# Moving the first batch's maxima, the query products and the weight pieces in the prologue of an attention and expert kernel

## The chip, the cores and the metric

The kernel runs on one core of a Trainium2 chip. The metric is the device time of one execution in microseconds. Engines are named as the profile names them: PE (matmuls; PEld its weight loads), DVE, ACT, POOL (elementwise work), SP (issues most DMAs). Each works through its own queue in order; semaphores join them.

## What is computed

One transformer layer for 8 batches of 512 tokens of width 256, with a context of the same shape. Of the reference, cut:

```
h   = layernorm(x)                                  # 8 x 512 x 256
qp  = h @ Wq.T                                      # query product
idx = argmax(qp @ ctx.T, axis=-1)                   # scores: each token chooses one context row
mk, mv = split(ctx[idx] @ Wkv.T)                    # 16 wide each, shared by all 16 heads
attn = softmax(qh @ mk.T / 4)                       # 16 heads of width 16
x   = x + tanh(g0) * ((attn @ mv) merged @ Wc.T)
h   = layernorm(x)
gate = h @ gate_w                                   # best 2 of 8 experts, softmax weights
x   = x + tanh(g1) * sum over the 2 of w * (gelu(h @ w1 + b1) @ w2 + b2)
```

## The kernel before

Only chosen context rows matter as keys, so the kernel counts how often each is chosen, packs the used ones into 192 slots and weights them by their counts. For each batch the work goes through these steps, in the names of the code and the trace:

- DVE's statistics of x (`x_stats`), POOL's `rstd` and normalising (`x_in`), PE's transposes (`turn_x`), ACT's copy (`turned`);
- PE's query product, two halves of 128 columns (`project`, into `ps_e0` and `ps_e1`), ACT's copy of each half (`q_t`), ACT's high halves (`query_hi`), POOL's low halves (`query_lo`), and SP's store of both (`queries`) and load into the stacked form `q_st` (`stack`, which holds SP until the load has landed);
- PE's scores, four tiles; DVE's search of each (MAX8 and FIND_INDEX8, `top`, `top_at`), and a mask of the chosen rows (`chosen_keys`: on DVE for the first batch, on POOL for the others);
- PE's counts, DVE's used keys, PE's ranks, DVE's positions, POOL's `values` and `places` (places on DVE for the first batch), PE's packing (`pack`, L1263 and L1268), ACT's `packed_keys`, which writes `k_st` and `v_st`;
- the maxima: 32 tiles of 128 x 384 logits (`logits_b`, L1280, bf16), of which DVE takes the row maxima (`take_max`, L987, `row_max`); then DVE splits them, PE turns them, DVE copies them (`max_t`) and SP stores them into the last rows of the stack (`store_max`), so that the next logits come out with the maximum subtracted;
- the logits (L1300, L1304), ACT's exponentials (L805), PE's weighted sums (L1317), then the layer's output, the gate and the scatter to expert queues. After all batches come the experts.

The order is written out by hand. All engines run the same loop over p = −4 to 7 and 32 steps each (`each_step`); a batch has its x loaded in p = b − 4, its query product in p = b − 3, its scores to packing in p = b − 2, the second part of its maxima in p = b − 1 and its logits in p = b. A table of step numbers for each engine (L407 to L427) says at which step an engine issues what; in one step the order is that of the `if`s in the engine's loop. Maxima tiles go one a step, beginning 7 steps before the end of p = b − 2 (`MAX_EARLY`), so that 7 tiles of a batch stand before the step in which the batch before has its first logits. While p < 0 the tiles and the scores go round four PSUM banks (`ps_d0, ps_d1, ps_a0, ps_a1`); from p = 0 the tiles have `ps_d` alone and the logits `ps_a` (`ring`). A tile can't be written before DVE has read the one four places earlier.

The experts' weights are brought in by 32 pieces of 512 KB: SP loads one into one of two stages (`load_piece`), ACT casts its high half (`piece_hi`, L849), POOL subtracts the low half (`piece_lo`, L706, 128 x 1024). `W_AT` gives the step of `piece_hi` for some p, POOL's follows one step later, SP's load of the piece after the next three steps later, which waits until the low half has freed the stage. DVE also copies the gate's 8 columns into a wide tile (`gate_wide`) before its loop, for which it waits for `tanh_g`.

## Time and profile before

| | |
|---|---|
| three runs | 923.81, 924.6, 925.47 us |
| median | 924.6 us |
| profiled execution | 923.9 us, its span 922.1 us |
| PE, DVE, ACT, POOL busy | 87%, 56%, 40%, 46% |

The span runs from the first to the last instruction; the profiled execution's time has 1.8 us more around it. Rows of the timeline give a start and a duration in us, and in brackets how long the engine had been idle and what ended that. The chain of waits is followed back from the last instruction, so that its rows add up to the span. Times in both are from the start of the span.

### The profile page before, as it was taken

The numbers are of one execution on the slowest core, as the hardware profiler recorded it, in microseconds if no ns is written. First come the engines' busy times: TensorE is split into PE (matmuls) and PEld (weight loads), VectorE is DVE, ScalarE is ACT, GpSimd is POOL, SyncE is SP. The second block draws the span as 40 slices with busy tenths as digits, with TensorE's granted clock in tenths as the row PEclk, the third lists the DMA queues.
The fourth block names the chain that finished last, engine by engine and source line by source line (L and its number), as shares of the span: only waits on it lengthen the run. The fifth ranks groups of instructions, "written<-read, shape, count | busy, mean of one in ns | idle before, by whom it ended". The sixth has DMA issues, their size and how long they took to land.

```text
span 922.1 us, 20046 instructions
## 1 busy us (share of the span) xinstructions
PE 801.9 (87%) x6326; PEld 547.1 (59%) x6327; DVE 521.0 (56%) x1582; ACT 370.3 (40%) x772; POOL 427.6 (46%) x469
## 2 busy tenths in 40 slices
PE   3785899989897998888778868999999999999994
PEld 1333344435353443443347657899888888899773
DVE  4585576667767567776444873544444544444441
ACT  1222363735435363566653612433333333333331
POOL 4596363755666546443614753333333333333322
PEclk9886899979899898989989989999999999999998
DMA  5554333353624334224425342322222333322300
GB/s 173 129 122 139 60 92 80 117 104 93 128 95 109 64 114 105 69 70 136 138 88 160 54 127 46 59 47 46 44 46 44 55 53 50 48 42 36 44 12 1
DMA packets 62798, 74.64 MB, mean 81 GB/s; under 512 B 6401, under 2 KB 56449, under 8 KB 62593
## 3 DMA queue, kind: packets, MB, share of 16 engines
q1 hardware_dynamic: 49424, 56.74, 24.0%
q0 software_dynamic: 13296, 16.92, 10.7%
q8 instruction: 42, 0.69, 0.3%
q14 instruction: 36, 0.29, 0.1%
HBM read 46.75 MB, written 27.55 MB: 81 GB/s over the span
## 4 chain that ended last, share of the span: by engine, by line
PE 66%; DVE 12%; ACT 6%; issue 6%; POOL 5%; DMA 3%; DVEq 1%; SPq 1%; ACTq 0%; POOLq 0%
PE ps_o L2578 20%; PE ps_d L2562 9%; PE ps_a L2562 9%; PE ps_d L1237 6%; PE ps_o L1317 5%; PE ps_d L1280 3%; PE ps_e L1212 3%; PE ps_e L1342 3%; PE ps_a L1300 2%; PE ps_e L1195 2%; DVE row_max L987 2%; PE ps_r L2548 1%; ACT prob L805 1%; ACT rows L827 1%; PE ps_a L1304 1%
## 5 line engine op out<-in xcount | busy, mean ns | idle before, releaser
L2578 PE MATMUL ps_o<-w_split,hidden 128*128 x1136 | 192.2, 276 | 13.4 <-DVE y L2534 8.4
L805 ACT ACTIVATE prob<-ps_a 128x512 f32<-128x512 f32 x192 | 112.9, 603 | 188.0 <-PE ps_a L1300 109.8
L987 DVE TENSOR_REDUCE row_max<-ps_d 128x2 f32<-128x384 f32 x237 | 127.8, 551 | 58.8 <-PE ps_d L1280 57.4
L2578 PE MATMUL ps_o<-w_split,h_lo 128*128 x568 | 156.6, 276 | 0.0
L2473 POOL DMA_INDIRECT out<-y,token_at x71 | 118.5, 1669 | 42.3 <-POOL token_at L2471 30.9
L2578 PEld LDWEIGHTS ps_o<-w_split,hidden 128*128 128x128 bf16 x1136 | 112.1, 99 | 30.2 <-issue 15.3
L2520 DVE TENSOR_TENSOR h_lo<-hidden 128x512 bf16<-128x512 f32 (+1 forms) x156 | 101.0, 686 | 25.5 <-ACT hidden L2489 24.7
L2534 DVE TENSOR_TENSOR y<-ps_o,b_all 128x512 f32<-128x512 f32 (+1 forms) x39 | 25.1, 644 | 155.6 <-PE ps_o L2578 148.7
L1280 PE MATMUL ps_d<-k_st,w_split 96*128 96x192 bf16 x474 | 84.4, 267 | 26.4 <-DVE row_max L987 19.8
L2562 PE MATMUL ps_a<-x_hi,w_split 128*128 128x256 bf16 (+1 forms) x624 | 104.4, 265 | 0.0
L2562 PE MATMUL ps_d<-x_hi,w_split 128*128 128x256 bf16 (+1 forms) x624 | 103.6, 264 | 0.1
L2469 POOL TENSOR_TENSOR token_f<-tails,ones_f 128x2 f32<-128x2 f32 (+1 forms) x39 | 7.7, 197 | 206.0 <-DVE y L2537 203.7
L706 POOL TENSOR_TENSOR w_split<-w_stage,w_split 128x1024 bf16<-128x1024 f32 x32 | 68.9, 2177 | 54.8 <-ACT w_split L849 54.8
L2480 ACT CAST x_hi<-ps_r 128x512 bf16<-128x512 f32 (+1 forms) x39 | 21.4, 548 | 168.6 <-PE ps_r L2548 168.6
L2489 ACT ACTIVATE hidden<-ps_d,bias 128x256 f32<-128x256 f32 (+1 forms) x156 | 62.4, 452 | 62.1 <-PE ps_d L2562 62.1
L1280 PEld LDWEIGHTS ps_d<-k_st,w_split 96*128 96x128 bf16 x474 | 39.7, 103 | 78.2 <-DVE row_max L987 31.9
L2562 PE MATMUL ps_a<-x_lo,w_split 128*128 128x256 bf16 (+1 forms) x312 | 81.9, 263 | 0.0
L1317 PE MATMUL ps_o<-prob,v_st 128*32 128x512 f32 x512 | 76.8, 675 | 5.5 <-issue 4.1
L2562 PE MATMUL ps_d<-x_lo,w_split 128*128 128x256 bf16 (+1 forms) x312 | 81.4, 263 | 0.0
L2489 ACT ACTIVATE hidden<-ps_a,bias 128x256 f32<-128x256 f32 (+1 forms) x156 | 62.4, 452 | 35.5 <-PE ps_a L2562 35.5
L700 POOL DMA_INDIRECT queue<-rows,slot x64 | 63.9, 999 | 19.4 <-issue 17.1
L2562 PEld LDWEIGHTS ps_a<-x_hi,w_split 128*128 x624 | 60.7, 97 | 9.4 <-issue 1.2
(242 smaller groups left out, 1307.1 us busy)
## 6 DMA issues: line engine op xcount, KB each, us to landing
w_stage<-w SPq DMA_DIRECT2D x32, 512.0 KB, 4.5
xg<-queue SPq DMA_DIRECT2D x31, 260.0 KB, 2.9
w_split<-q_split SPq DMA_DIRECT2D x24, 256.0 KB, 8.0
x_in<-x SPq DMA_DIRECT2D x8, 512.0 KB, 4.3
ctx_sb<-ctx_t SPq DMA_DIRECT2D x8, 512.0 KB, 3.9
x<-x SPq DMA_DIRECT2D x8, 512.0 KB, 4.3
q_split<-q_hl SPq DMA_DIRECT2D x16, 256.0 KB, 3.4
out<-x SPq DMA_DIRECT2D x8, 512.0 KB, 5.0
```

Of the source, the lines that this page charges most:

```text
L700: pool.indirect_dma_start(k.queue[:], bass.IndirectOffsetOnAxis(ap=slot[:, t, c:c + 1], axis=0), rows[:, t, :], None).then_inc(scattered, 16)
L706: g.tensor_tensor(lo, stage, hi, ALU.subtract).then_inc(w_lo, 1)
L805: a.activation(prob[n % 2][:, j, :], ps_a[i % 2][:], ACT.Exp, scale=SCALE).then_inc(exp_ready, 1)
L987: v.tensor_reduce(row_max[:, t, 2 * pair:2 * pair + 2], bank[:, 0:2 * SLOTS].rearrange("p (h r) -> p h r", h=2), AX.X, ALU.max).then_inc(m ...
L1237: last = t_.matmul(ps_da[n][:], q_t[:, kt, t * P:(t + 1) * P], ctx_sb[:, kt, :], start=(kt == 0), stop=(kt == KT - 1))
L1280: last = t_.matmul(ps_da[n][:, c * SLOTS:(c + 1) * SLOTS], q_st[m % 3][0:ROW_MAX, 2 * pair + c, t * P:(t + 1) * P], k_st[0:ROW_MAX, m % 3, ...
L1317: last = t_.matmul(ps_o[j * VW:(j + 1) * VW, :], values, probs, start=(key_tile == 0), stop=(key_tile == SLOT_TILES - 1))
L2473: pool.indirect_dma_start(k.out_rows, bass.IndirectOffsetOnAxis(ap=token_at[:, t:t + 1], axis=0), y[s][:, t, :], None, bounds_check=B * L ...
L2489: last = nc.scalar.activation(hidden[s][:, f, 0:width(i)], ps_h[n][:, c, 0:width(i)], ACT.Gelu, bias=bias[s][:, f:f + 1])
L2520: nc.vector.tensor_tensor(h_lo[s][:, both, tokens], hidden[s][:, both, tokens], h_hi[s][:, both, tokens], ALU.subtract).then_inc(h_lo_read ...
L2562: last = nc.tensor.matmul(ps_h[n][:, c, 0:width(i)], k.w1_split[:, bass.ds(e, 1), part, kt, f].rearrange("p a f -> p (a f)"), xs[s][:, kt, ...
L2578: last = nc.tensor.matmul(ps_y[:, t, :], hs[s][:, f, token], k.w2_split[:, bass.ds(e, 1), part, f, :].rearrange("p a d -> p (a d)"), start ...
```

## The change

The sizes and the number of instructions stay. The first batch's maxima go two tiles a step for the first 12 steps and then one a step (`FIRST_MAX`), still from the 26th step of p = −2 on, so that they end in step 12 of p = −1; their split, turn, copy and store move from steps 25 to 28 into steps 13 to 16 (`max_steps`). For p < 0 the query product's halves move from steps 16 and 17 to 19 and 25, behind ranks (18), and behind packing (22) for the second half; ACT's copies, high halves, POOL's low halves and SP's store follow (`query_steps`). In p = −2 and −1 ACT's high halves of the weight pieces move from steps 4, 10, 18, 26 to 13, 15, 22, 28, and with them POOL's low halves and SP's loads. The gate columns move from ahead of DVE's loop into p = −3.

```diff
-        W_AT = {-2: (4, 10, 18, 26), -1: (4, 10, 18, 26), 6: (4, 10, 18, 26), 7: (2, 8, 14, 20)}
+        W_AT = {-2: (13, 15, 22, 28), -1: (13, 15, 22, 28), 6: (4, 10, 18, 26), 7: (2, 8, 14, 20)}
...
+        def query_steps(p):
+
+            return ((19, 25), (20, 26), 27, 28, 29) if p < 0 else (PE_PROJECT, ACT_QUERY, ACT_QUERY_HI, POOL_QUERY_LO, SP_QUERIES)
+
+        def max_steps(m):
+
+            return (13, 14, 14, 16) if m == 0 else (DVE_SPLIT_MAX, PE_TURN_MAX, DVE_COPY_MAX, SP_MAX)
...
-        def max_tile(p, step):
+        FIRST_MAX = [2] * 12 + [1] * 8
+
+        def max_tiles(p, step):
 
             m, tile = divmod(p * STEPS + step + MAX_EARLY, STEPS)
-            return (m + 1, tile) if is_batch(m + 1) else None
+            if m >= 0:
+                return [(m + 1, tile)] if is_batch(m + 1) else []
+            n = (p + 1) * STEPS + step + MAX_EARLY
+            return [(0, sum(FIRST_MAX[:n]) + i) for i in range(FIRST_MAX[n])] if 0 <= n < len(FIRST_MAX) else []
...
-                if step == SP_QUERIES and is_batch(p + 3):
+                if step == query_steps(p)[4] and is_batch(p + 3):
                     queries(p + 3)
...
-                if step == SP_MAX and is_batch(m):
+                if is_batch(m) and step == max_steps(m)[3]:
                     store_max(m)
...
-                if step == POOL_QUERY_LO and is_batch(p + 3):
+                if step == query_steps(p)[3] and is_batch(p + 3):
                     query_lo(p + 3)
...
-            dve.wait_ge(dve_ready, 2)
-            dve.wait_ge(pool_ready, 1)
-            dve.wait_ge(tanh_ready, 1)
-
-            chain.then(v.memset(gate_wide[:], 0.0))
-            v.tensor_copy(gate_wide[:, :, 0:E], k.gate_sb[:]).then_inc(dve_ready, 1)
+            def gate_columns():
+                dve.wait_ge(pool_ready, 1)
+                dve.wait_ge(tanh_ready, 1)
+                chain.then(v.memset(gate_wide[:], 0.0))
+                v.tensor_copy(gate_wide[:, :, 0:E], k.gate_sb[:]).then_inc(dve_ready, 1)
...
             n_d = 0
+            dve.wait_ge(dve_ready, 2)
             for p, step in each_step():
...
+                if step == 0 and p == -3:
+                    gate_columns()
...
-                row_tile = max_tile(p, step)
-                if row_tile:
+                for row_tile in max_tiles(p, step):
                     take_max(*row_tile, (ps_d + ps_a)[ring(p, n_d)][:])
                     n_d += 1
...
-                row_tile = max_tile(p, step)
-                if row_tile:
+                for row_tile in max_tiles(p, step):
                     logits_b(*row_tile, ring(p, n_d))
                     n_d += 1
...
-                if step in PE_PROJECT and is_batch(p + 3):
-                    project(p + 3, PE_PROJECT.index(step))
+                if step in query_steps(p)[0] and is_batch(p + 3):
+                    project(p + 3, query_steps(p)[0].index(step))
```

ACT's queries and high halves, the split, the copy and the turn of the maxima are edited in the same way. The changed file's lines are 13 or 14 higher.

How the order moves is seen at three places. On PE, from the counts of the first batch (`chosen`) through the second batch's query product (`wq_sb`), ranks (`used`) and packing (`key_cols`, `value_cols`) to the first maxima tiles (`k_st`, two matmuls a tile), before:

```order
L1247 MATMUL ps_r<-ones_bf,chosen 128x1 x16
L1212 MATMUL ps_e<-turned,wq_sb 128x512 x4
L1255 MATMUL ps_r<-used,before 128x4
L1256 MATMUL ps_r<-used,ones_bf 128x4
L1263 MATMUL ps_e<-chosen,key_cols 98x192 x4
L1268 MATMUL ps_e<-value_cols,chosen 128x17 x8
L1268 MATMUL ps_e<-value_cols,chosen 64x17 x16
L1280 MATMUL ps_d<-k_st,w_split 128x192 x4
```

and after:

```order
L1261 MATMUL ps_r<-ones_bf,chosen 128x1 x16
L1269 MATMUL ps_r<-used,before 128x4
L1270 MATMUL ps_r<-used,ones_bf 128x4
L1226 MATMUL ps_e<-turned,wq_sb 128x512 x2
L1277 MATMUL ps_e<-chosen,key_cols 98x192 x4
L1282 MATMUL ps_e<-value_cols,chosen 128x17 x8
L1282 MATMUL ps_e<-value_cols,chosen 64x17 x16
L1294 MATMUL ps_d<-k_st,w_split 128x192 x4
L1226 MATMUL ps_e<-turned,wq_sb 128x512 x2
```

The ranks stand directly behind the counts, half of the product ahead of packing, and the other half behind the first two maxima tiles. Behind it come 23 more tiles before the second batch's first scores (25 in all; before, 13 tiles stood ahead of them); the same pattern stands in p = −1, there with the second half of the product behind the first tile of the second batch. On ACT, from the second batch's `turned` to the first batch's packed keys (`k_st`, `v_st`), before:

```order
L760 COPY turned<-ps_e 128x512
L761 COPY turned<-ps_e 128x512
L768 COPY q_t<-ps_e 128x512 x2
L849 CAST w_split<-w_stage 128x1024
L774 CAST q_hl<-q_t 128x2x512
L780 ACTIVATE k_st<-ps_e,key_add,key_mul 98x192
```

and after:

```order
L773 COPY turned<-ps_e 128x512
L774 COPY turned<-ps_e 128x512
L862 CAST w_split<-w_stage 128x1024
L781 COPY q_t<-ps_e 128x512
L862 CAST w_split<-w_stage 128x1024
L793 ACTIVATE k_st<-ps_e,key_add,key_mul 98x192
```

The third weight piece's cast (the second cast shown after) stands directly ahead of the packed keys, and the second copy and the high halves of the queries behind them. On POOL, from the choice of the second batch's last tiles (`best`, `chosen<-column,best`) to its places (`chosen<-column,position`), before:

```order
L648 TENSOR_SCALAR chosen<-column,best 128x512
L706 TENSOR_TENSOR w_split<-w_stage,w_split 128x1024
L647 CAST best<-top_at 128x1
L648 TENSOR_SCALAR chosen<-column,best 128x512
L652 TENSOR_TENSOR value_f<-kv,count 128x4x16
L654 COPY value_f<-count 128x4
L657 CAST value_cols<-value_f 128x4x17
L658 TENSOR_TENSOR value_cols<-value_f,value_cols 128x4x17
L706 TENSOR_TENSOR w_split<-w_stage,w_split 128x1024
L668 TENSOR_SCALAR chosen<-column,position 128x192 x4
```

and after:

```order
L660 CAST best<-top_at 128x1
L661 TENSOR_SCALAR chosen<-column,best 128x512
L719 TENSOR_TENSOR w_split<-w_stage,w_split 128x1024 x2
L665 TENSOR_TENSOR value_f<-kv,count 128x4x16
L667 COPY value_f<-count 128x4
L670 CAST value_cols<-value_f 128x4x17
L671 TENSOR_TENSOR value_cols<-value_f,value_cols 128x4x17
L681 TENSOR_SCALAR chosen<-column,position 128x192 x4
```

Two weight pieces stand between the last choice and the values, and none between the choices or ahead of the places. On SP the loads of the second batch's context and the third batch's x stand ahead of two weight pieces behind the first stack; before, they stood second and fourth of the four.

## Rows read from the trace of the kernel before

**Rows 1.** Chain that ended last, 0 to 130: start, us, what
```profile
31.95 8.00 DMA w_split<-q_split
...
40.96 0.46 SPq L515
...
67.35 2.08 POOL w_split L706
...
78.70 2.12 POOL w_split L706
...
80.82 2.97 POOL chosen L668 x4
...
83.83 0.88 PE ps_e L1263 x4
...
89.40 3.09 DMA w_split<-max_t
...
92.54 0.61 PE ps_a L1300
...
98.69 1.93 PE ps_d L1237 x4
```

**Rows 2.** Timeline: start, us, engine line op out<-in [idle <-releaser]; the start
```profile
3.69 6.95 POOL L636 MEMSET w_split<- 96x4096 f32 x2
...
11.38 0.24 POOL L673 TENSOR_SCALAR variance<-moments 128x4 f32<-128x4 f32 x1 [0.74 <-DVE moments L1023]
```

**Rows 3.** Timeline, to the first batch's first maxima tile, 39 to 49 us
```profile
39.17 5.95 PE L1212 MATMUL ps_e<-turned,wq_sb 128*128 128x512 f32 x8
...
45.63 1.05 ACT L849 CAST w_split<-w_stage 128x1024 bf16<-128x1024 f32 x1
...
47.98 0.51 ACT L780 ACTIVATE k_st<-ps_e,key_add,key_mul 98x192 bf16<-98x192 f32 x1 [0.36 <-PE ps_e L1268]
...
48.89 0.49 PE L1280 MATMUL ps_d<-k_st,w_split 96*128 96x192 bf16 x4 [0.95 <-issue]
```

**Rows 4.** DMA issues near 41 us: count, KB each, us to landing
```profile
ctx_sb<-ctx_t SPq DMA_DIRECT2D x1, 512.0 KB, 4.7
w_stage<-w SPq DMA_DIRECT2D x1, 512.0 KB, 5.6
```

**Rows 5.** Timeline, maxima tiles, second batch's scores, 49 to 68 us
```profile
49.87 0.99 DVE L987 TENSOR_REDUCE row_max<-ps_d 128x2 f32<-128x384 f32 x2
...
54.72 3.28 PE L1237 MATMUL ps_d<-ctx_sb,q_t 128*128 128x512 f32 x4
...
55.42 0.56 DVE L987 TENSOR_REDUCE row_max<-ps_d 128x2 f32<-128x384 f32 x1
...
58.04 0.70 DVE L945 MAX8 top<-ps_d 128x8 f32<-128x512 f32 x1 [2.07 <-PE ps_d L1237]
...
67.09 0.69 DVE L946 FIND_INDEX8 top_at<-top,ps_a 128x8 uint32<-128x512 f32 x1
```

**Rows 6.** Timeline, choice, third batch's product, values, 69 to 75 us
```profile
69.67 1.56 POOL L648 TENSOR_SCALAR chosen<-column,best 128x512 bf16<-128x512 f16 x1
...
72.01 3.13 PE L1212 MATMUL ps_e<-turned,wq_sb 128*128 128x512 f32 x4
...
73.17 0.29 POOL L652 TENSOR_TENSOR value_f<-kv,count 128x64 f32<-128x64 f32 x1 [1.94 <-DVE used L958]
...
73.99 0.31 POOL L658 TENSOR_TENSOR value_cols<-value_f,value_cols 128x68 bf16<-128x68 f32 x1
```

**Rows 7.** Busy time by stretch; third from last: PE's granted clock
```profile
54.00:55.00 1.00, 0.95 (x5) 0.44 (x4) 1.00 (x4) 0.00 (x0) 1.00 (x2) 0.50 0.00 0
...
72.00:73.00 1.00, 1.00 (x4) 0.48 (x3) 0.71 (x3) 0.00 (x0) 0.00 (x0) 0.50 1.04 395
...
99.00:100.00 1.00, 1.00 (x3) 0.38 (x2) 0.00 (x0) 0.00 (x0) 0.00 (x0) 1.00 1.17 116
```

**Rows 8.** Timeline, the second batch's first maxima tiles, 86 us
```profile
86.64 0.80 PE L1280 MATMUL ps_d<-k_st,w_split 96*128 96x192 bf16 x4 [0.20 <-issue]
```

More of the change, by code:

```diff
@@ L857, in _ @@
                     turned_x(p + 3)
-                if step in ACT_QUERY and is_batch(p + 3):
-                    query(p + 3, ACT_QUERY.index(step))
-                if step == ACT_QUERY_HI and is_batch(p + 3):
+                if step in query_steps(p)[1] and is_batch(p + 3):
+                    query(p + 3, query_steps(p)[1].index(step))
+                if step == query_steps(p)[2] and is_batch(p + 3):
                     query_hi(p + 3)
@@ L1128, in _ @@
                     x_moments_of(p + 4)
-                if step == DVE_SPLIT_MAX and is_batch(m):
+                if is_batch(m) and step == max_steps(m)[0]:
                     split_max(m)
-                if step == DVE_COPY_MAX and is_batch(m):
+                if is_batch(m) and step == max_steps(m)[2]:
                     copy_max(m)
@@ L1420, in _ @@
                     turn_rows(e)
-                if step == PE_TURN_MAX and is_batch(m):
+                if is_batch(m) and step == max_steps(m)[1]:
                     turn_max(m)
```

## Prediction

> **What bounds the kernel now.** The change touches only what runs before the first logits, so that stretch alone is read, first in the chain of waits from 0 to 130 us [rows 1]. The reader is to see how often the step that ends last there is a single DMA or one engine's queue: the stack load that holds SP until 31.95 + 8.00 = 39.95, the weight pieces of POOL at 67.35 and 78.70, the placing of the second batch's keys at 80.82, the packing at 83.83, the store of the first batch's maxima at 89.40, and the first logits at 92.54. The timelines then give durations. I cut the stretch at six points: first maxima tile on PE 48.89 [rows 3]; first MAX8 of the second batch's scores 58.04; end of the fourth search, 67.09 + 0.69 = 67.78 [rows 5]; packing 83.83; first logits 92.54; third batch's first scores 98.69 [rows 1]. The stages last 48.9, 9.1, 9.7, 16.1, 8.7 and 6.2 us. From 98.69 on both kernels issue the same rows, and what waits there waits for its predecessors and not for the clock on the wall, so a shift at 98.69 is carried to the end whole.
>
> **Stage 1, start to the first tile.** The gate columns no longer hold DVE for tanh_g. What is late next is POOL: its memsets end at 3.69 + 6.95 = 10.64, and the variance that started at 11.38 [rows 2] can start some 0.7 us earlier, no more. Query products and ranks are exchanged: before, the first batch's ranks stood behind the second batch's whole product (39.17, 5.95 for eight records, [rows 3]); now half of it, about 3 us, stands there, and behind the ranks. Packing can so begin near 44, by half the product and a copy behind 39.17. But ACT has the third weight piece in its queue ahead of the packed keys, and that piece is loaded third after the stack: SP is free at 39.95 less the 0.35 that I take of the 0.7 (the low halves on POOL now stand behind two normalised tiles), 39.6; the third transfer is issued 1.0 later (40.96 against 39.95, [rows 1]) and lands 5.6 after its issue [rows 4]: 46.2. The cast takes 1.05, so the key copy starts at 47.3 instead of 47.98, and the tile 0.91 behind it as before (48.89 − 47.98, [rows 3]): 48.2. **−0.7 us**; 0 if the load starts no earlier. The x of the third batch moves from fourth to second in line (4.7 after issue, [rows 4]), so its statistics no longer hold the first maximum.
>
> **Stage 2, first tile to the second batch's first search.** PE had 13 tiles ahead of the first scores and now has 25. DVE's pitch is (55.42 + 0.56 − 49.87)/13 = 0.47 us a tile [rows 5], and PE keeps ahead of it even at half clock (0.80 for two tiles at 86.64, [rows 8]), so 12 more cost 5.6. Behind the first two tiles stands the second half of the query product, four records, on which DVE waits in full. At 72.01 such four took 3.13 [rows 6] at a granted clock of 0.50, that is 1.2 GHz [rows 7]; the same shape at full clock took 1.93 (98.69, [rows 1], clock 1.00 at 99). PE is nearly idle from about 45.5 to 48.2, as it was before 72.01, so I take 3.1. Gained back is DVE's late start: 49.87 came 0.98 behind the tile, now about 0.4, −0.6. **+8.1 us**, down to +6.9 with the product at full clock. The first scores ran at half (54.72, 3.28, clock 0.50); I leave them so; at full they give 1.35 back.
>
> The Trainium skill, "TensorE: Matmul & The Clock Gate", Part 1, says that the throttled state is the default and that sustained activity releases it, so that products behind an idle stretch start at half rate. The clock at 72 agrees. The rule speaks against a product set between two idle stretches; by it both moved halves run at half clock, and without it the sum below would be 2.4 us less.
>
> **Stage 3, the four searches.** DVE has the same rows in the same order with seven tiles between and behind: 0.
>
> **Stage 4, last search to packing, 16.05 us before.** POOL's choice of the fourth tile was held by a weight piece (67.35, 2.08), the ranks by the whole product, and the placing by another piece (78.70, 2.12). Now the choice follows at once, 1.56 [rows 6] and with the copy ahead of it and hand-overs 1.9; then come two weight pieces in a row, 2 x 2.12 = 4.25; values, 73.99 + 0.31 − 73.17 = 1.13 [rows 6]; placing 2.97 [rows 1]; hand-overs 0.3. Sum 10.55. Counts and used keys (POOL waited 1.94 for them at 73.17), then ranks and positions, hide behind the two pieces, and half the product (3.1) and its copy behind pieces, values and placing. ACT's high half of the second piece waits for the turned x, which PE issues about with the last search: ready before POOL wants it. **−5.5 us**, ±0.5. Were the pieces not there, values would start about 3 us earlier; this is the cover that the change doesn't give.
>
> **Stage 5, packing to the first logits, 8.71 before.** Packing to the first tile of the second batch stays 86.64 − 83.83 = 2.81 [rows 1, 8]. The maxima are stored long before, which takes the 3.09 of the store out of the chain. But behind that first tile now stands the other half of the third batch's product (0.4 + 3.1), and behind it six tiles whose maxima DVE must take before the bank of the logits is free: 0.45 to the first, 0.55 for it, 5 x 0.47. Sum 9.7: **+1.0 us**; with the product at full clock −0.2.
>
> **Stage 6, first logits to the next scores, 6.15 before**, all at half clock until 98. The product just ahead may bring PE's clock up. At full clock I bound the gain between 0 and 2.0 (a third of the stage; its exponentials and hand-overs don't shrink), and take **−0.9**, since tiles alone between 49 and 54 didn't hold the clock up (0.50 at 54, [rows 7]).
>
> Weight pieces moved cost the SP queue nothing else: the maxima's store waits on SP behind the context and x loads, which are issued before the maxima exist. The second batch's stack now waits for one more piece's low half, and is issued near 61 and loaded some nine later, 18 us before its first tile.
>
> **Sum:** −0.7 + 8.1 + 0 − 5.5 + 1.0 − 0.9 = **+2.0 us**. The profiled execution took 923.9 us (span 922.1, 1.8 around it); the median of the three shown is 924.6. 923.9 + 2.0 = 925.9, and against the median **926.6 us**. About 0.2%, 1.85 us, is what a measurement of this kernel can tell from no change.
>
> **The rivals.** *Same, by the clock:* the product of stage 5 and the first logits run at full clock: −0.7 + 8.1 − 5.5 − 0.2 − 2.0 = −0.3, 924.3 us. For it: four records of f32 work at 72 were followed by full clock. Against it: six tiles follow, and at such tiles the clock fell to half by 54. *Same, by the piece:* the third weight piece lands earlier than I have it, so that the key copy follows packing. Then the tile is near 46.4 instead of 48.2, and the sum +0.2: 924.8 us. Against it: the transfers before it landed one behind the other [rows 4]. *Faster:* PE holds the full clock from the first packing on. Then stage 2 loses 1.2 and 1.35, stage 5 another 1.2, stage 6 the whole 2.0: −0.7 + 5.5 − 5.5 − 0.2 − 2.0 = −2.9, 921.7 us. It decides where the product behind the second tile takes under 2.5 us and the first scores under 2.6. Against it are PE's idle stretches on both sides of packing. *Slower still:* the second scores run at half too (+1.35) and nothing comes back in stage 6 (+0.9): +4.3, 928.9 us. *The change doesn't do what it says:* the first tile comes no sooner, since the piece's landing decides; this is in the forecast.
>
> **How the numbers follow.** The forecast gets 0.40, slower still 0.08, the two that end the same 0.28 and 0.08, faster 0.16. So faster by over 0.2% 0.16, within 0.2% 0.36, slower by over 0.2% 0.48. Slower and same hold most of the chance; the forecast's own range, from stage 6 at −2.0 to stages 1 and 6 at 0, is 925.5 to 928.2. The range that leaves out no more than 2 in 10 reaches from 922.0, which takes in most of the faster case by its milder clocks, to 929.8, above the worst case by the ±0.5 of stage 4 and some.
>
> **What would show it.** Right: the key copy directly behind a weight cast that waited for its load, near 47.3; 25 tiles at 0.47 with a hole of about 3 us behind the second; the first search near 65.5; two weight pieces between POOL's last choice and the values; the maxima's store landed by about 81; first logits near 95.4. Wrong: the key copy before 46, the first search before 63.5, or values that start before the second piece; and a first-logits time that isn't carried to the end.

## The result, and the profile after

The kernel before has a median of 925.1 us over seven runs, the three above and four more. The changed kernel takes **928.2 us** (seven runs, 927.7 to 930.7), a ratio of **1.0047**, 95% interval 1.0037 to 1.0058: slower by some 4.3 us by this ratio and by 3.0 us by the medians, where 2.0 was forecast. Its profiled execution took 929.6 us, its span 927.9.

The chain of waits of the changed kernel from 40 to 106 us (start, us, what; line numbers 12 to 14 higher than before). It answers [rows 1]:

```profile
45.19 3.43 issue
48.62 0.80 PE ps_d L1294 x4
49.42 3.47 PE ps_e L1226 x4
...
62.77 3.75 PE ps_d L1251 x4
...
77.22 1.56 POOL chosen L661
78.78 2.18 POOL w_split L719 x2
...
84.21 3.00 POOL chosen L681 x4
87.26 0.53 PE ps_e L1277 x4
...
90.18 3.49 PE ps_e L1226 x4
...
97.05 0.39 PE ps_a L1314
...
102.98 2.90 PE ps_d L1251 x4
```

The store of the maxima of 89.40 [rows 1] is gone from the chain. The stack load of 31.95 isn't listed in it either, but it still decides: the 3.43 us of "issue" are PE's wait for the first batch's key copy, which stands on ACT behind a cast that waited 3.49 us for its weight piece (46.76 and 47.71 below), and SP could issue that load only behind the stack's, after 39.92. New in the chain are half products, at 49.42 behind the first two tiles and at 90.18 behind the second batch's first; the two weight pieces at 78.78 stand in a row. The timeline has what waits behind these (idle time and its cause in brackets), and answers [rows 3, 5, 6]:

```profile
39.92 0.38 SPq L556 DMA_DIRECT2D ctx_sb<-ctx_t  x1
...
46.76 1.04 ACT L862 CAST w_split<-w_stage 128x1024 bf16<-128x1024 f32 x1 [3.49 <-DMA w_stage<-w]
...
47.71 0.51 ACT L793 ACTIVATE k_st<-ps_e,key_add,key_mul 98x192 bf16<-98x192 f32 x1
...
53.24 1.02 DVE L999 TENSOR_REDUCE row_max<-ps_a 128x2 f32<-128x384 f32 x2 [3.08 <-PE ps_a L1294]
...
66.56 0.70 DVE L957 MAX8 top<-ps_d 128x8 f32<-128x512 f32 x1 [2.54 <-PE ps_d L1251]
...
79.14 0.84 SPq L570 DMA_DIRECT2D w_split<-max_t  x1
...
94.03 0.56 DVE L999 TENSOR_REDUCE row_max<-ps_d 128x2 f32<-128x384 f32 x1 [3.25 <-PE ps_d L1294]
```

DVE's two idle times of 3.08 and 3.25 us, both released by a tile behind a half product, are the holes. The clock in single microseconds (third from last) answers [rows 7]:

```profile
49.00:50.00 1.00, 1.00 (x4) 0.59 (x3) 0.87 (x2) 0.00 (x0) 1.00 (x2) 0.50 0.00 0
...
54.00:55.00 1.00, 0.75 (x7) 0.23 (x4) 1.00 (x3) 1.00 (x2) 0.34 (x1) 1.00 0.00 0
62.00:63.00 1.00, 0.94 (x5) 0.39 (x4) 1.00 (x3) 0.00 (x0) 0.00 (x0) 0.50 0.68 70
...
95.00:96.00 1.00, 0.38 (x3) 0.11 (x2) 1.00 (x4) 1.00 (x2) 0.55 (x1) 1.00 0.00 0
99.00:100.00 1.00, 1.00 (x6) 0.28 (x3) 0.73 (x2) 0.85 (x2) 1.00 (x2) 0.50 0.99 351
103.00:104.00 1.00, 1.00 (x2) 0.48 (x3) 0.00 (x0) 0.00 (x0) 0.00 (x0) 0.50 0.96 123
```

Behind each half product the clock was up (1.00 at 54 and 95), and each time it was back at 0.50, which is 1.2 GHz, before the next scores: at 62 under tiles, at 99 under the first logits. Both half products and the first scores of the second batch ran at half, those of the third batch until near 105.

Cut at the six points of the prediction, the stages of every kernel run, as differences from the kernel before, in us, from one profiled execution each (the sixth cut is the start of PE's first record, 98.62 before). The last columns: all up to there; up to the MAX8 of the third batch's first scores (100.64 before); and of the runs the median and the ratio to the kernel before. The ratio is the recorded one, against runs of the kernel before from the same session (medians 924.9 to 925.2); it differs from the quotient of the medians by up to 0.14%, 1.3 us. One execution carries its own clock: in *gate columns only* no row of the scores was edited, yet the second batch's first scores are 0.5 us longer than before and the third batch's 1.8 us. Differences of that size in a single stage need a second sign.

| kernel | 1 | 2 | 3 | 4 | 5 | 6 | sum | MAX8 | median | ratio |
|---|---|---|---|---|---|---|---|---|---|---|
| forecast | −0.7 | +8.1 | 0 | −5.5 | +1.0 | −0.9 | +2.0 | | 926.6 | |
| changed | −0.3 | +8.8 | +0.6 | −5.7 | +1.1 | −0.2 | +4.3 | +5.3 | 928.2 | 1.0047 |
| gate columns only | −0.7 | +1.6 | +0.7 | +0.3 | 0.0 | +0.2 | +2.2 | +4.0 | 924.7 | 0.9999 |
| pieces only | +0.1 | −0.6 | +0.4 | −3.6 | +1.5 | +0.2 | −1.9 | −1.3 | 923.5 | 0.9971 |
| tiles only | −0.3 | +6.5 | +0.2 | −0.2 | −1.9 | +0.2 | +4.5 | +5.4 | 931.2 | 1.0071 |
| product only | −0.9 | +3.3 | +0.2 | −4.1 | +1.3 | −0.7 | −1.1 | −1.0 | 923.6 | 0.9996 |
| tiles undone | −0.3 | +1.2 | +0.2 | −5.4 | +2.3 | 0.0 | −2.1 | −2.1 | 924.2 | 0.9988 |
| pieces undone | −1.6 | +8.2 | +0.2 | −5.2 | +1.1 | +0.2 | +2.8 | +3.1 | 928.1 | 1.0037 |
| product undone | −0.6 | +5.6 | +0.8 | −5.7 | −2.4 | +0.2 | −2.0 | −1.1 | 924.6 | 0.9991 |
| product ahead of packing | 0.0 | +5.5 | +0.8 | −5.6 | −2.2 | +0.2 | −1.4 | −0.6 | 921.5 | 0.9972 |
| changed, PE kept busy | −1.3 | +6.6 | +0.6 | −5.7 | −1.2 | +0.2 | −0.8 | −0.6 | 923.5 | 0.9984 |
| late pairs | −0.4 | −0.4 | +0.3 | −4.1 | −1.9 | +0.2 | −6.3 | −5.4 | 919.0 | 0.9927 |
| late pairs, four added | +3.0 | −0.1 | +0.7 | −4.1 | −2.7 | +0.2 | −3.0 | −2.7 | 914.9 | 0.9889 |
| late pairs, three added | −0.7 | −0.7 | 0.0 | −2.9 | −2.6 | +0.2 | −6.8 | −6.0 | 916.2 | 0.9911 |

### The profile page after: what moved, and what is told of

It is laid out like the page before. It is cut to its first block, busy times and chain, and to the rows that moved or that the text cites. A ratio compares the mean times of both kernels' runs of the same rounds, so it can differ in the third digit from the quotient of the medians.

```text
span 927.9 us, 20045 instructions
## 1 busy us (share of the span) xinstructions
PE 811.0 (87%) x6326; PEld 549.7 (59%) x6327; DVE 524.5 (57%) x1582; ACT 369.8 (40%) x772; POOL 427.4 (46%) x469
## 3 DMA queue, kind: packets, MB, share of 16 engines
HBM read 46.75 MB, written 27.55 MB: 80 GB/s over the span
## 4 chain that ended last, share of the span: by engine, by line
PE 69%; DVE 14%; ACT 6%; issue 6%; POOL 4%; DVEq 1%; DMA 0%; ACTq 0%; POOLq 0%
PE ps_o L2591 20%; PE ps_d L2575 9%; PE ps_a L2575 8%; PE ps_d L1251 6%; PE ps_o L1331 5%; PE ps_e L1226 4%; PE ps_d L1294 3%; PE ps_e L1356 3%; DVE row_max L999 3%; PE ps_a L1314 2%; PE ps_e L1209 2%; PE ps_r L2561 1%; ACT prob L818 1%; DVE top_at L958 1%; PE ps_a L1318 1%
## 5 line engine op out<-in xcount | busy, mean ns | idle before, releaser
L2591 PE MATMUL ps_o<-w_split,hidden 128*128 x1136 | 194.9, 278 | 11.6 <-DVE y L2547 6.7
L1294 PEld LDWEIGHTS ps_d<-k_st,w_split 96*128 96x128 bf16 x474 | 39.6, 103 | 81.2 <-DVE row_max L999 32.7
```

The lines of the kernel that those rows point to most:

```text
L1294: last = t_.matmul(ps_da[n][:, c * SLOTS:(c + 1) * SLOTS], q_st[m % 3][0:ROW_MAX, 2 * pair + c, t * P:(t + 1) * P], k_st[0:ROW_MAX, m % 3, ...
L2591: last = nc.tensor.matmul(ps_y[:, t, :], hs[s][:, f, token], k.w2_split[:, bass.ds(e, 1), part, f, :].rearrange("p a d -> p (a d)"), start ...
```

## The experiments

The first four undo one part of the change, or all but one.

**Tiles undone** (the rest as changed):

```diff
-        FIRST_MAX = [2] * 12 + [1] * 8
+        FIRST_MAX = [1] * 32
...
-            return (13, 14, 14, 16) if m == 0 else (DVE_SPLIT_MAX, PE_TURN_MAX, DVE_COPY_MAX, SP_MAX)
+            return (25, 26, 27, 28) if m == 0 else (DVE_SPLIT_MAX, PE_TURN_MAX, DVE_COPY_MAX, SP_MAX)
```

> The changed kernel with one edit undone: the first batch's maxima go one tile a step again and their store stands where it stood before. Theory (the twelve tiles ahead of the second batch's scores cost more than the earlier store gives back): the first search comes 12 x 0.47 = 5.6 us earlier than in the changed kernel, near 61.0; values and packing follow it, packing near 81.7; then the store of the maxima stands in the chain again and puts the first logits at about 8.7 to 10 us behind packing, 91 to 92. Against the kernel before -1 to 0 us (ratio 0.999 to 1.000), against the changed kernel some 4 us less. Rival 1 (the weight pieces cost it: the third one ahead of the packed keys, two ahead of the values): nothing of that is undone, so the time stays within 1 us of the changed kernel's, ratio near 1.004. Rival 2 (TensorE's clock: the products and first scores at half): the same, since both halves of the product still stand between idle stretches; ratio 1.003 to 1.005.

Measured: 924.2 us, ratio 0.9988 (0.9976 to 1.0000), 4.0 us under the changed kernel, as the theory had it; both rivals had at most 1 us. Its chain:

```profile
49.06 3.22 PE ps_e L1226 x4
...
56.90 1.95 PE ps_d L1251 x4
...
82.77 3.44 PE ps_e L1226 x4
...
87.32 3.11 DMA w_split<-max_t
```

The first scores come 5.9 us earlier, and here at full clock (1.95 for 3.75), so the first search is at 58.9 instead of 66.6: 5.6 by tiles, 1.8 by the clock. Both half products are still there, and behind the second one the store of the maxima is back in the chain: the stage before the first logits costs +2.3.

**Pieces undone:**

```diff
-        W_AT = {-2: (13, 15, 22, 28), -1: (13, 15, 22, 28), 6: (4, 10, 18, 26), 7: (2, 8, 14, 20)}
+        W_AT = {-2: (4, 10, 18, 26), -1: (4, 10, 18, 26), 6: (4, 10, 18, 26), 7: (2, 8, 14, 20)}
```

> The changed kernel with the weight pieces back at their old steps; maxima and products stay as changed. Theory: the key copy no longer stands behind the third piece's cast (46.76 in the changed kernel), so the first tile reaches PE near 46 instead of 48.6; the third batch's x is loaded last again, so its statistics hold DVE until some 50 us, under which the 3-us hole behind the second tile disappears: DVE is through the tiles 1 to 2.5 us earlier. Later POOL's pieces stand between the choices and ahead of the places again, which costs part of it back: 0 to +1.5 in the stage from the last search to packing. In all -1 to -2.5 us against the changed kernel, ratio to the kernel before 1.002 to 1.003. Rival (the pieces are what costs the 4 us): all of it comes back, ratio 0.999 to 1.001. Rival (the tiles alone cost it, pieces are neutral): ratio 1.004 to 1.005.

Measured: 928.1 us, ratio 1.0037 (1.0024 to 1.0050); by the medians nothing, by the stages 1.5 us less than changed, nearly all from the first tile, which comes at 47.26. The hole of 3 us behind the second tile stayed (PE's half product 48.05, 3.14, DVE's next maxima at 51.39), which the theory had hidden. The rival that the pieces cost the 4 us falls. Unlooked for was the fourth stage: with the pieces back between the choices and ahead of the places it still gained 5.2.

**Product undone:**

```diff
-            return ((19, 25), (20, 26), 27, 28, 29) if p < 0 else (PE_PROJECT, ACT_QUERY, ACT_QUERY_HI, POOL_QUERY_LO, SP_QUERIES)
+            return (PE_PROJECT, ACT_QUERY, ACT_QUERY_HI, POOL_QUERY_LO, SP_QUERIES) if p < 0 else (PE_PROJECT, ACT_QUERY, ACT_QUERY_HI, POOL_QUERY_LO, SP_QUERIES)
```

> The changed kernel with the query product for p < 0 back ahead of the ranks, both halves together; tiles, store and pieces stay as changed. Theory (each moved half is an uncovered wait of 3.0 to 3.5 us on DVE, once behind the second tile of the first batch and once behind the first tile of the second): the first search comes 3 us earlier, near 63.5, and the stretch from packing to the first logits is 3 us shorter, near 6.8; the ranks stand behind the whole product again, which costs 0 to 3 us between the last search and packing where two weight pieces cover most of it. In all -3 to -6 us against the changed kernel, ratio to the kernel before 0.998 to 1.001. Rival (tiles cost it, the product is neutral as it only changes places): ratio 1.004 to 1.005. Rival (clock: the product in one piece brings PE to full clock for the tiles and scores behind it): first scores under 2.6 us and ratio under 0.998.

Measured: 924.6 us, ratio 0.9991 (0.9976 to 1.0006), 3.6 us under the changed kernel by the medians and 6.3 by the stages. The holes are gone (second stage +5.6, about the twelve tiles, with first scores of 3.75; fifth −2.4, the store out of the chain), and the fourth stage keeps its −5.7, although the whole product stands ahead of the ranks again. The clock rival falls: the product in one piece did not keep the clock up until the scores.

**Gate columns only:** the three edits above together.

> Of the change only the gate columns' move from ahead of DVE's loop into p = -3; the rest is as in the kernel before. Every theory: POOL's variance starts at 10.6 instead of 11.4; how much of these 0.7 us reaches the first tile depends on the store and load of the first stack, between 0 (as in the changed kernel, where the stack landed as late as before) and 0.7. Ratio to the kernel before 0.9992 to 1.0005; above 1.002 the move of the gate columns itself would cost something that no theory has.

Measured: 924.7 us, ratio 0.9999 (0.9989 to 1.0009): nothing. In its profiled execution the first tile comes 0.7 earlier, and then the first scores run at 3.75 and the third batch's at 3.73 us; the 4.0 us that it is late at the MAX8 are gone at the end (923.4 against 923.9).

**One part alone.** Undoing the tiles and undoing the product each gave back nearly all; so the parts don't add up, and each was run alone. *Pieces only* (tiles and product undone):

> Of the change only the weight pieces and the gate columns; one maxima tile a step, their store and the query product as in the kernel before. Theory by stages: the gain of the stage from the last search to packing (-5.2 to -5.7 in every kernel so far that had any of the moved parts but the gate columns alone) comes with the pieces and needs nothing else; nothing is added ahead of the second batch's scores, where PE's clock decides between -1 and +1.6; packing to first logits as before. First tile near 48.3, packing near 78 to 80, first logits near 87 to 89, ratio to the kernel before 0.994 to 0.997. Rival (the gain needs the product out of the way of the ranks, or the tiles): packing near 83 to 84, ratio 0.999 to 1.001. Second rival (what the prologue gains or loses isn't carried to the end): packing near 79 but a ratio of 0.998 to 1.001.

Measured: 923.5 us, ratio 0.9971 (0.9957 to 0.9986). By the medians that is 1.4 us under the kernel before, by the ratio 2.7. The gain of the fourth stage is there without the other parts, but it is 3.6 and not 5.5: POOL had to wait for the places, as its timeline shows (POOL) with its chain (PE):

```profile
77.22 2.99 POOL L681 TENSOR_SCALAR chosen<-column,position 128x192 bf16<-128x192 f16 x4 [2.28 <-DVE position L981]
```

```profile
70.47 3.15 PE ps_e L1226 x4
...
73.95 1.88 PE ps_e L1226 x4
```

The first half of the product ahead of the ranks ran at half clock here (clock 0.50 from 71 to 73), so positions came 2.3 us behind POOL. In the kernel with only the product undone the clock was 1.00 from 65 to 83, and positions held POOL by 0.17 us.

*Tiles only* (pieces and product undone):

> Of the change only the maxima's tiles two a step with their store, and the gate columns; product and weight pieces as in the kernel before. Theory by stages: S2 +5.6 (12 tiles of 0.47), up to +1.5 more where the scores run at 3.75 instead of 3.28; S4 as before (16 us), since the pieces stand between the choices and ahead of the places; S5 -2.4, since the store is out of the chain; first logits near 95 to 97; ratio to the kernel before 1.002 to 1.005. Rival (two tiles a step and the earlier store pay for themselves, and the product alone is to blame): ratio 0.998 to 1.001.

Measured: 931.2 us, ratio 1.0071 (1.0056 to 1.0085), more than the theory's upper end; by the stages +4.5, by the MAX8 +5.4. The tiles are the costly part, and their rival falls.

*Product only* (tiles and pieces undone):

> Of the change only the query product's moved halves with what follows them, and the gate columns; tiles, store and weight pieces as in the kernel before. Theory by stages: S2 +1 to +3.5 for the half behind the first tile, less where the third batch's statistics on DVE cover it; S4 0 to -1.5, since the ranks come free but two pieces still stand in POOL's way; S5 +2.3, since the other half stands behind the second batch's first tile and the store of the maxima waits behind that; first logits near 93.5 to 96.5; ratio to the kernel before 1.002 to 1.005. Rival (the product is neutral by itself, and only with the pairs of tiles it costs): ratio 0.999 to 1.001.

Measured: 923.6 us, ratio 0.9996 (0.9979 to 1.0012), no difference, where the theory had 1.002 to 1.005. That is the rival's number but not its reason: the product isn't neutral. The second stage cost 3.3, as expected, and the fifth 1.3 instead of 2.3, but the fourth gave 4.1 instead of 0 to 1.5, with the pieces at their old places:

```profile
69.83 2.09 POOL w_split L719
...
72.15 1.59 POOL chosen L661
73.78 0.58 PE ps_r L1261 x16
...
76.88 2.04 DVE offset L980
...
79.20 3.01 POOL chosen L681 x4
```

Before, a whole product stood ahead of the ranks, positions came at 77.7, and POOL was then held by a piece until 80.82 [rows 1]. That piece was late because of the product too: its cast stood on ACT behind the copies of the product's halves, and POOL waited 4.40 us for it (timeline of the kernel before, ACT and POOL):

```profile
77.09 0.58 ACT L768 COPY q_t<-ps_e 128x512 f32<-128x512 f32 x1 [1.33 <-PE ps_e L1212]
77.57 1.05 ACT L849 CAST w_split<-w_stage 128x1024 bf16<-128x1024 f32 x1
...
78.70 2.12 POOL L706 TENSOR_TENSOR w_split<-w_stage,w_split 128x1024 bf16<-128x1024 f32 x1 [4.40 <-ACT w_split L849]
```

Moving the product frees the ranks and this cast; moving the pieces takes the piece out of the way. Without the product there, places begin 1.6 us earlier although the searches end 2.5 later. So most of the 5.5 us of the fourth stage can be had by moving the product *or* the pieces (4.1 and 3.6 alone, 5.2 and 5.7 with the tiles moved too); the second one to be moved adds little: with the tiles moved, 0.5 for the pieces, and 0 for the product, which ran at full clock there.

**Product ahead of packing** (else as changed):

```diff
-            return ((19, 25), (20, 26), 27, 28, 29) if p < 0 else (PE_PROJECT, ACT_QUERY, ACT_QUERY_HI, POOL_QUERY_LO, SP_QUERIES)
+            return ((19, 20), (20, 21), 22, 24, 25) if p < 0 else (PE_PROJECT, ACT_QUERY, ACT_QUERY_HI, POOL_QUERY_LO, SP_QUERIES)
```

> The changed kernel with the second half of the query product for p < 0 put behind ranks and the first half, ahead of packing, where the first half already stands; tiles, store and weight pieces stay as changed. Theory by stages (the cost of the product is where its halves stand, not how long they take): the holes of 3 us behind the first batch's second tile and behind the second batch's first tile go, as they went when the product was put back ahead of the ranks (S2 +5.6 instead of +8.8, S5 -2.4 instead of +1.1). The second half then stands ahead of packing in both batches: for the first one packing moves from 43.4 to about 47, so that the key copy follows it and no longer the third weight piece, 0 to +1.2 at the first tile; for the second the product of up to 7 us stands beside two weight pieces, values and places of 8.3 us together, 0 to +1. In all ratio to the kernel before 0.997 to 1.001. Rival (the product costs by its half clock wherever it stands): ratio 1.003 to 1.005.

Measured: 921.5 us, ratio 0.9972 (0.9957 to 0.9986). Both holes go and the fourth stage keeps its gain: it is the place of the second half behind the tiles that costs, not its length.

**Late pairs.** If twelve tiles ahead of the scores cost and the pieces leave DVE and PE idle later, the pairs belong there (product undone as above):

```diff
-        FIRST_MAX = [2] * 12 + [1] * 8
+        FIRST_MAX = [1] * 20 + [2] * 6
...
-            return (13, 14, 14, 16) if m == 0 else (DVE_SPLIT_MAX, PE_TURN_MAX, DVE_COPY_MAX, SP_MAX)
+            return (19, 20, 20, 22) if m == 0 else (DVE_SPLIT_MAX, PE_TURN_MAX, DVE_COPY_MAX, SP_MAX)
```

> The changed kernel with the query product for p < 0 back ahead of the ranks, and with the pairs of maxima tiles placed last instead of first: one tile a step until 20 are done (13 of them ahead of the second batch's first scores, as in the kernel before), then two a step for six steps, while the second batch's keys are chosen and the weight pieces split on POOL; the store of the maxima follows three steps later. Theory by stages: nothing is added ahead of the scores (0 to +1.6 by PE's clock instead of +5.6), the gain between last search and packing stays (-5 to -5.7), and the store is out of the chain of the first logits (-2.4). First logits near 84.5 to 87, ratio to the kernel before 0.991 to 0.995. Rival (late tiles only move the wait, as DVE takes 5.6 us of them beside the second batch's used keys and positions): packing 2 to 4 us later than that, ratio 0.996 to 0.999. Second rival (not carried): first logits near 86, ratio 0.998 to 1.001.

Measured: **919.0 us**, ratio **0.9927** (0.9908 to 0.9945), some 6.8 us under the kernel before by the ratio and 5.9 by the medians; first logits at 86.05. The theory holds but for the fourth stage, −4.1 instead of −5 to −5.7. The rival's mechanism, tiles beside the used keys, has a part in that, with another one on top. The timeline of *late pairs* (DVE and POOL):

```profile
71.57 1.84 DVE L970 TENSOR_SCALAR used<-count 128x4 bf16<-128x4 f32 x1
```

```profile
69.18 4.22 POOL L719 TENSOR_TENSOR w_split<-w_stage,w_split 128x1024 bf16<-128x1024 f32 x2
```

`used` over four columns takes 0.17 us elsewhere. Here it ends at 73.41, with POOL's two pieces (73.40), and the ranks, positions and places wait behind it.

**PE kept busy.** The clock's part is told by matmuls that nobody needs: in the changed kernel, two behind the first batch's packing and one ahead of the second's.

```diff
+            def filler(n):
+                for _ in range(n):
+                    t_.matmul(ps_o[:], wq_sb[:, 0, 0:P], turned[:, 0, :], start=True, stop=True)
...
                 if step == PE_PACK and is_batch(s):
+                    if s == 1:
+                        filler(1)
                     pack(s)
+                    if s == 0:
+                        filler(2)
```

> The changed kernel with three matmuls of the size of the query product's added on PE, into a bank that nobody reads before it is written anew: two behind the first batch's packing, while the key copy waits for a weight piece, and one ahead of the second batch's packing, while POOL places. Clock theory (the 3.5 us of each moved half and the 2.96 to 3.75 of the first scores are half-clock times that come from PE's idle stretches just ahead): with the stretches filled the half behind the second tile takes 1.9 to 2.5 instead of 3.5, first scores 1.9 to 2.6, and the half behind the second batch's first tile about 1.9: 2 to 4 us off the changed kernel, ratio to the kernel before 1.000 to 1.002. Rival (the clock doesn't rise for so few, or the time is set elsewhere): durations stay at 3.3 to 3.75, or the fillers delay packing by 0 to 1, ratio 1.004 to 1.006.

Measured: 923.5 us (916.7 to 928.4 in twelve runs), ratio 0.9984 (0.9960 to 1.0009), 4.7 us under the changed kernel. Its chain:

```profile
44.94 1.91 PE ps_o L1398 x4
...
48.10 1.75 PE ps_e L1226 x4
...
59.57 3.75 PE ps_d L1251 x4
...
86.53 1.83 PE ps_e L1226 x4
```

The half products take 1.75 and 1.83 instead of 3.47 and 3.49, as the clock theory has it, and the whole execution (920.5 us) had a mean granted clock of 0.951, where the changed kernel's seven had 0.935 to 0.942. But this trace doesn't show that the added matmuls brought the clock up. It had risen before the first of them (single microseconds, third from last the clock):

```profile
43.00:44.00 1.00, 0.28 (x5) 0.29 (x5) 0.00 (x0) 0.58 (x1) 0.00 (x0) 0.68 1.09 378
44.00:45.00 1.00, 1.00 (x28) 0.95 (x27) 0.76 (x3) 0.00 (x0) 0.00 (x0) 1.00 1.09 345
```

In the changed kernel it was 0.50 from 37 to 53, although PE has the same instructions up to there. That is a difference between the two executions; the added matmuls, 1.91 us between packing and the first tile, can at most have kept the clock up until the product. The first scores still took 3.75: tiles alone did not hold it up. The twelve executions go with the clock, but for one: with 0.951 to 0.954 four took 916.7 to 920.5, with 0.939 to 0.942 three took 926.9 to 928.4, and one with 0.946 took 926.9 as well. By medians the matmuls give back 4.7 us, more than the two products' 3.4 and as much as the whole loss, and the intervals of the two ratios don't overlap. That the added matmuls shorten the time is shown; that they do it by the clock at these two products rests on one trace.

**Late pairs with added matmuls,** two behind the first packing and two ahead of the second:

> The kernel with the late pairs of tiles (product ahead of the ranks, pairs last) and four added matmuls of the size of the query product's into a bank that nobody reads before it is written anew: two behind the first batch's packing, two ahead of the second batch's, both while PE waits. Clock theory: what the half clock still costs there (first scores 3.34 at 53.85, tiles 0.8 at 82.04, first logits and weighted sums from 86 to 95, all at 0.50) comes partly back: first scores 1.9 to 2.6, packing to first logits 5.5 to 6.5 instead of 6.82, first logits to the next scores 4.5 to 6 instead of 6.25; 1.5 to 4 us less than without them, ratio to the kernel before 0.988 to 0.992. Rival (the clock rises behind the added matmuls but tiles alone don't hold it until the scores, as with the fillers in the changed kernel, where the scores still took 3.75): 0 to 1.5 us, ratio 0.991 to 0.994.

Measured: **914.9 us** (914.5 to 922.1, five runs), ratio **0.9889** (0.9874 to 0.9903). The profiled execution was the one of 922.1, with a mean clock of 0.945; the others had 0.951 to 0.952. What it shows is a cost: the added matmuls ran at half and held the first tile back to 51.89 (chain; packing itself came only at 47.22, as the whole product ahead of it ran at half too):

```profile
48.45 3.61 PE ps_o L1398 x4
```

So that trace doesn't explain the median. The last kernel has one instead of two there:

> The kernel with the late pairs of tiles and the added matmuls, with one of them instead of two behind the first batch's packing (two stay ahead of the second batch's packing). In the profiled execution with two, the added ones ran at half clock (3.61 from 48.45) and held the first tile back to 51.89; its mean granted clock was 0.945 and its time 922.06, while the four others had 0.951 to 0.952 and 914.5 to 917.6. Clock theory: one takes 0.9 to 1.8 and ends ahead of the key copy, the first tile comes at 48.5 again, and the mean granted clock is 0.948 to 0.952 with a time of 0.988 to 0.991 of the kernel before. Rival (one is too little to bring the clock up, or the four executions were quick for another reason): mean granted clock 0.940 to 0.945 and ratio 0.991 to 0.994, as without any.

Measured: 916.2 us (915.8 to 918.1), ratio 0.9911 (0.9897 to 0.9925), mean clock 0.949 to 0.953 in all five, against 0.940 to 0.945 in the six of *late pairs*. The first tile is at 48.15. But up to the third batch's scores it gains only 0.4 us on *late pairs*, as the added matmuls ahead of the second packing cost about what they bring (chain):

```profile
47.20 1.05 PE ps_o L1398 x2
...
76.16 3.51 PE ps_o L1398 x4
79.66 0.43 PE ps_e L1277 x4
```

The rest of the 4.0 us between the two profiled executions lies later, in stretches where both issue the same rows. From 240 to 270 us *late pairs* and this kernel, in this order (third from last the clock):

```profile
240.00:270.00 30.00, 28.83 (x168) 14.48 (x161) 20.00 (x50) 10.47 (x19) 16.97 (x19) 0.87 0.35 74
```

```profile
240.00:270.00 30.00, 28.83 (x176) 14.43 (x175) 19.52 (x49) 10.70 (x20) 18.06 (x23) 1.00 0.40 115
```

Why added matmuls before 80 us should keep the clock up at 250 isn't shown by any run. The interval of the four lies just below that of *late pairs* without any, that of the three overlaps with it.

## Why the prediction was right in sign and short in size

*The mechanism* was right: 25 tiles ahead of the scores, holes behind the moved halves, two pieces in a row, and the store out of the chain. The first search was put at 65.5 and came at 66.6, the first logits at 95.4 and came at 97.05. The 2.3 us that the sum lacks at the sixth cut are four terms, each short by half a microsecond or so. That the cut's +4.3 equals the 4.3 us by the ratio is partly chance: the profiled executions lie 1.5 us above the median of the changed kernel and 1.2 below that of the kernel before.

- *Stage 1, −0.7 forecast, −0.3 measured.* POOL's variance started at 10.64, 0.74 earlier, as forecast. But SP was free for the next loads at 39.92 instead of 39.6: the store of the queries was issued 0.5 us earlier (27.55 for 28.05) and the load of the stack behind it 0.2 later (31.27 for 31.06): the gain was lost between the store's issue and its landing (2.7 us at the median, 2.3 before). The cast waited for its load, and the key copy stood right behind it, as foreseen (46.76, 47.71; forecast 47.3 for the copy).
- *Stage 2, +8.1 forecast, +8.8 measured.* The pitch of 0.47 held. The half product stood 3.47 us in the chain instead of 3.1: at 72.01 [rows 6] the clock had risen before the product ended (0.77 in the microsecond from 74), here it did not. The scores took 3.75 instead of 3.28 for the same reason: before [rows 5], the clock rose from 57 on, while they ran.
- *Stage 3, 0 forecast, +0.6 measured.* The same rows in the same order, but PE's keys and values (L1236) ran at half clock, 0.84 in the chain. Where they did (0.81 to 1.01, *gate columns only*, *product undone* and *PE kept busy* among them), the stage is 0.6 to 0.8 longer; where they took 0.57, it is between 0 and 0.4. The step left the clock out.
- *Stage 6, −0.9 forecast, −0.2 measured.* The clock was up at 95, as assumed, but it fell at 98, under the logits; and the third batch's first scores then ran mostly at half, 2.90 in the chain instead of 1.93, which adds 1.0 behind the last cut.

*Stage 4* (−5.5, measured −5.7) and *stage 5* (+1.0, measured +1.1) were sized right. The reasons given for stage 4 were only half right: it was told as a gain of the moved pieces and of the free ranks together, but the single runs show that either edit brings most of it, as the piece ahead of the places was itself late by the product. Read so before, the change would have been seen to pay for one gain twice: the product's move costs 3.2 us in stage 2 and 3.4 in stage 5 (*changed* against *product undone*), for a gain that the pieces bring too.

*Of the rivals,* "slower still" gave +4.3 and 928.9, near the result, but partly by luck: nearly nothing came back in stage 6, as it has it, but the second scores, which it puts at half, ran at full clock (1.91 from 67.79); its 1.35 us stand in for what the products, the first scores and stages 1 and 3 lacked. "Same, by the clock" fell with the half product at 90.18, which took 3.49, and "same, by the piece" with the key copy, which stood behind the cast. "Faster" hung on a product under 2.5 us and on first scores under 2.6. With the added matmuls the product took 1.75 and the time fell by 4.7 us, though the scores still took 3.75: what it says of the product is real, but its condition was absent from the changed kernel.

*That a shift at 98.69 is carried whole* holds in the mean and not in one execution: from the third batch's MAX8 to the end the change in the profiled executions altered by −2.8 to +1.3 us, and by −4.6 in *gate columns only*; the mean of the thirteen is −0.5. It goes with the later dips of the clock, as at 240 to 270 above: added up in stretches of 5 us as time times what the clock lacks to 1.00, they come to 34.6 us from there to the end before, 29.7 in *gate columns only*, 31.3 in *changed, PE kept busy* and 36.4 in *late pairs*, whose remainders are 4.6 and 2.8 us shorter and 1.3 longer.

## What to carry to other kernels

An earlier store is worth only what it takes out of the chain (2.4 us here); if its work is put ahead of something that the chain needs, that work counts in full (12 × 0.47), and it belongs into the idle time that another wait leaves, as the late pairs show. Before two moves are added up, ask whether they remove the same wait. And a long product set between two waits should be costed at both clocks: the half behind the first tiles took 3.47 us in one trace and 1.75 in another.

## What was not expected of the hardware

Matmuls that nobody needs shortened the time: in the changed kernel by 4.7 us at the medians. In the profiled execution PE's clock was at 1.00 ahead of the first two of them and still at 1.00 for the product behind them; without them, in another execution, it was 0.50 in both places.

A VectorE instruction of 0.17 to 0.35 us took up to 2.05 us beside one of POOL's weight pieces, and ended with the piece. In the changed kernel (timeline, DVE and POOL):

```profile
30.52 1.65 DVE L962 TENSOR_SCALAR chosen<-column,best 128x512 bf16<-128x512 f16 x1
...
34.60 0.35 DVE L962 TENSOR_SCALAR chosen<-column,best 128x512 bf16<-128x512 f16 x1
...
80.03 0.86 DVE L970 TENSOR_SCALAR used<-count 128x4 bf16<-128x4 f32 x1
80.93 2.05 DVE L972 TENSOR_SCALAR unused<-used 128x4 f32<-128x4 bf16 x1
```

```profile
27.51 2.42 POOL L694 TENSOR_SCALAR x_in<-x_in,moments,rstd 128x256 f32<-128x256 f32 x2
29.90 2.12 POOL L719 TENSOR_TENSOR w_split<-w_stage,w_split 128x1024 bf16<-128x1024 f32 x1
...
78.75 4.20 POOL L719 TENSOR_TENSOR w_split<-w_stage,w_split 128x1024 bf16<-128x1024 f32 x2
```

30.52 + 1.65 = 32.17 and 29.90 + 2.12 = 32.02; 80.93 + 2.05 = 82.98 and 78.75 + 4.20 = 82.95. Beside POOL's normalising (`x_in`) the same mask took its 0.35, at 28.03. The Trainium skill, "SBUF — State Buffer", section "Who interferes with whom", says that VectorE in a two-port mode, which `tensor_scalar` can enter, and GpSimd exclude each other on a shared port for a whole instruction. The trace agrees for the subtraction of the pieces, with the ends above; it doesn't for `x_in`, beside which 0.35 us were enough, so the measurement decides: in these rows POOL's subtraction of two tensors held VectorE, its scaling of one did not; whether the mask ran in a two-port mode no row shows. On the path to the first logits this stood in *late pairs* and, with the 2.04 of `offset`, in *product only*.
